# Causal attention with relative keys and a mixture of experts: skewed-key reads moved behind the next quad's write, keys 14 steps ahead, expert weights loaded one at a time

## The chip, the cores and the metric

The kernel runs on one core of one Trainium2 chip. The metric is device time in microseconds (us), lower is better. The core has a matrix engine (PE, its weight loads PEld), a vector engine (DVE), an activation engine (ACT), GpSimd (POOL) and a sync engine (SP), which here issues every DMA of the program, one after another, in the order of its program.

## What is computed

One pre-norm transformer block in fp32, over x of 8 x 512 x 128, with 16 heads of 8 elements:

```python
qkv = x @ w_attn                                   # x is the layer norm of the input
rel = jnp.tril(idx[:, None] - idx[None, :])        # distance t - s, 0 above the diagonal
att = einsum('bhtd,bhsd->bhts', q, k) * scale + einsum('bhtd,tsd->bhts', q, embk[rel])
att = softmax(where(causal, att, -inf))
y = einsum('bhts,bhsd->bhtd', att, v) + einsum('bhts,tsd->bhtd', att, embv[rel])
x = x + y @ w_proj
x = x + ffn(layernorm(x))   # softmax gate, 2 of 8 experts, and 2 shared experts
```

The tables embk and embv have 128 rows, so a distance over 127 takes row 127. The last row of each table is taken out of the tables and put into k and v beforehand, and only the near 128 distances are left to a special path.

## The kernel before

**The work.** A first part normalises x and makes q, k and v of all batches in four groups, and writes them to HBM as bf16 parts (`qk_rows`) and fp32 values (`v_dram`). Then comes attention, until about 610 us, then the expert layer (`expert_part`) to the end.

**Attention.** Four pairs of batches are worked through. Each has four rows of 128 queries, in the order ROWS = [2, 0, 1, 3]; row i sees (i+1) x 128 keys. A row of a pair has 32 heads, in 8 quads of 4 heads, so there are 128 quads, q = 0 to 127. A quad is cut into steps (UNITS): 1 head per step in rows 2 and 3, 2 in row 1, 4 in row 0, so a quad has 4, 1, 2 and 4 steps in rows 2, 0, 1 and 3, and there are 352 steps in all. `FIRST[q]` is the first step of quad q. I call the rows 2 and 3, with 4 steps a quad, the wide rows.

In a step m, PE transposes probabilities of step m-3 (L771), does whatever the table OPS holds for that step, and multiplies q by k for step m+1 (L759). DVE adds the near part to the scores of the step and takes their minimum in one instruction per head (L979, of the negated scores), ACT takes the exponential (L906). Copies of transposed probabilities go to ACT (L895) and DVE (L964) in turn. POOL, L720 and L724, folds the near probabilities, PE applies v (L788) and the relative values (L804).

**The near part, which the change is about.** For quad q:

1. PE multiplies q by the 128 relative keys (`rel`, L746) at step `REL_AT[q]`; ACT copies the product to SBUF (`rel_copy`, L884, 5 buffers).
2. SP writes it to HBM, `put_rel`, issued at L628: 256 KB into one of 8 slots with a pitch that is off by one element per partition. That skews it.
3. SP reads it back from the slot, `get_near`, issued at L636: 512 KB (256 KB in row 0) into one of NEAR = 5 buffers. Ahead of this DMA, SP waits for the write of the same quad to have landed (`w_out`), and for the buffer to be free (quad q-5 done on DVE).
4. The first L979 of quad q on DVE waits until the read has landed.

`rel_slots` sets how many steps the relative keys run ahead: 8 in rows 0 and 1, 10 in rows 2 and 3. `READ_AT` sets the step at which SP's program has the read. SP has no clock of its own: it goes through the steps m, and in each does first the reads of that step, then the writes, then other DMAs (rows of the first part, q, k and v of the next pair, residuals, stores). What paces it are its waits: a write waits until ACT has copied the product, a read until its own write has landed.

**Weights.** `load_weights` (L1127) issues the gate, its bias and w1, w3, w2 of the experts, 640 KB each, in one go, 8 steps after quad 32, the first of the second pair. They are first used in the expert layer.

Of the kernel before, what the change touches and what calls it, by code (L numbers as in the profile page):

```python
# [16 lines left out]
NI = T // P  # L17
# [9 lines left out]
QUADS = NH // 4  # L27
# [14 lines left out]
NQ = GI * QUADS  # L42
NEAR = 5
RSLOTS = 5
WSLOTS = 8
PROBS = 5
MINS = 32
MISC = 3
MISC_BANK = 5
# [7 lines left out]
FIRST = [UNITS.index((q, 0)) for q in range(NQ)] + [NU]  # L57


def row(q):  # L60

    return ROWS[q // QUADS % NI]
# [15 lines left out]
def rel_slots():  # L78

    at = []  # L80
    for q in range(NQ):
        ahead = 8 if row(q) <= 1 else 10
        reload = last(q - QUADS) + 4 if q // QUADS % NI == 0 and q >= QUADS else 0
        at.append(max(reload, FIRST[q] - ahead, *at[-1:]))
    return at
# [64 lines left out]
OPS, BANK, BEFORE, LAST = schedule()  # L150
SLOT_OF = {op: m for m in range(SLOTS) for op in OPS[m]}
REL_AT = [SLOT_OF["rel", q] for q in range(NQ)]
READ_AT = [max(REL_AT[q] + 3, FIRST[max(q - NEAR + 1, 0)]) if REL_AT[q] else 0 for q in range(NQ)]


def on_act(m):
# [333 lines left out]
def attention_part(nc, t, x, w_attn, w_proj, e_k, e_k127, e_k127h, e_v, e_v127, part_of_row, qk_rows, v_dram, w_slots,  # L490
                   x1_dram, experts_of):
    with ExitStack() as ctx:
# [31 lines left out]
        experts = experts_of(ctx, t, ps_all)  # L524
# [63 lines left out]
        with nc.Block() as block:  # L588

            @block.sync  # L590
            def _(sp):
# [23 lines left out]
                def load_v(g):  # L615
                    if g >= 2:
                        sp.wait_ge(av_done, NI * QUADS * (g - 1))
                    sp.dma_start(vb[:, g % 2, :, :], v_dram[:, g * GB * NI:(g + 1) * GB * NI, :]).then_inc(v_in[g % 2], 16)
# [53 lines left out]
                for m in range(SLOTS):  # L672
                    for q in range(NQ):
                        if READ_AT[q] == m > 0:
                            get_near(q)
                    for q in range(NQ):
                        if REL_AT[q] == m > 0:
                            put_rel(q)
                    for k in range((m - 2) * 3 // 2, (m - 1) * 3 // 2):
                        if 0 <= k < 2 * (2 * NPART + 1):  # L680
                            first["rows"](sp, 2 + k // (2 * NPART + 1), [k % (2 * NPART + 1)])
                    for q in range(NQ):
                        if m == last(q) + 1 and q // QUADS % NI == NI - 1 and q // QUADS // NI + 1 < G:
                            load_qk(q // QUADS // NI + 1, q % QUADS)
                        if m == last(q) + 8 and q % (NI * QUADS) == 0 and q // QUADS // NI + 1 < G:
                            if q == 0:
                                sp.wait_ge(*first["second_rows"])
                            elif q == NI * QUADS:
                                first["wait_rows"](sp)
                                experts["weights"](sp)  # L690
                            load_v(q // QUADS // NI + 1)
                    for e in range(GI - 1):
                        if m == SLOT_OF["yt", e, 0]:
                            load_residual(e)
                        if m == SLOT_OF["pj", e] + 3:
                            store(e)
                    if m == FIRST[NQ - QUADS]:
                        sp.wait_ge(av_done, NI * QUADS * (G - 1))
                        for j in range(3):
                            wait_stored(sp, j)  # L700
                            experts["load"](sp, j)
# [344 lines left out]
def expert_part(nc, ctx, t, ps, x1_dram, gate_w, gate_bias, w1, w3, w2, out):  # L1046
# [8 lines left out]
    w1_sb = w1_v.rearrange("p (m c) -> p m c", m=NM)  # L1055
# [24 lines left out]
    w_in = sem("w2_in")  # L1080
# [41 lines left out]

        return [j for j in range(1, CHUNKS) if prepared_at(j)[what] == step]

    def load_weights(sp):
        for dst, src in ((gw, gate_w), (gb, gate_bias), (w1_sb, w1), (w3_sb, w3), (w2_sb, w2)):
            sp.dma_start(dst, src).then_inc(w_in, 16)  # L1127

    def load_tokens(sp, j):
        sp.dma_start(x1c[j % 3], x1_tiles[:, CT * j:CT * (j + 1), :]).then_inc(x1c_in[j % 3], 16)  # L1130
# [312 lines left out]
```

## Time and profile before

| | before |
|---|---|
| time, median of 3 runs | 851.3 us (845.1 to 855.38) |
| the profiled execution | 854.7 us, of which the span is 853.0 us |
| PE busy | 717.1 us, 84% of the span |
| DVE / ACT / POOL busy | 70% / 60% / 30% |
| data moved | 140.32 MB, 164 GB/s over the span |
| attention steps | from about 60 to about 610 us |
| expert layer | from about 612 to 853 us |

The busy time of PE is that of pipelined matmuls and is not a measure of PE at its peak. An engine with idle time before an instruction has the name of what ended the wait beside it. SP's rows are issues of DMAs; a transfer itself goes on after its issue.

### The profile page before, as it was taken

The page shows a single profiled execution, that of the slowest core. Times are in us where ns is not written, and L with a number is a line of the kernel's source. Part 1 is how long each engine was busy: PE and PEld are TensorE (multiplying, and loading weights), DVE is VectorE, ACT ScalarE, POOL GpSimd, SP SyncE. Part 2 cuts the span into 40 slices and gives each one's busy share as a digit, 9 for nine tenths or more (in the row PEclk, how much of TensorE's full clock was granted, in tenths as well). Part 3 has the DMA queues.
Part 4 walks back from the last instruction along what each step waited for, and adds up shares of the span by engine and source line. Part 5 has one row for each costly group of instructions (what it writes and reads, how often), then busy time and mean ns, then how long its engine had stood idle before and what let it go on. Part 6 is the DMA issues. An engine that isn't in the chain of part 4 may idle for free. (4 is left out here: it accounts for less than half of the span.)

```text
span 853.0 us, 27128 instructions
## 1 busy us (share of the span) xinstructions
PE 717.1 (84%) x10368; PEld 522.4 (61%) x10368; DVE 594.8 (70%) x2036; ACT 512.4 (60%) x1031; POOL 255.2 (30%) x253
## 2 busy tenths in 40 slices
PE   3667569898597888877989777988799999999998
PEld 2345447676465766655768565767666666666665
DVE  6835458878477696767778657867746767766776
ACT  2565478687486685877768667758733434534331
POOL 8333236433235442435534333543300000000000
PEclk9877799999999898999999999989979999999999
DMA  9789989677788667569767658864200000000000
GB/s 312 235 277 286 351 259 273 183 211 207 233 244 241 188 181 215 169 202 290 220 170 217 180 159 250 259 190 128 74 2 20 25 26 25 13 13 13 13 13 13
DMA packets 116687, 140.32 MB, mean 164 GB/s; under 512 B 8848, under 2 KB 83088, under 8 KB 116368
## 3 DMA queue, kind: packets, MB, share of 16 engines
q1 hardware_dynamic: 116560, 138.59, 53.9%
q8 instruction: 84, 1.38, 0.7%
q14 instruction: 43, 0.35, 0.1%
HBM read 82.26 MB, written 56.30 MB: 162 GB/s over the span
## 5 line engine op out<-in xcount | busy, mean ns | idle before, releaser
L979 DVE CUSTOM_DVE_ANT_0 ps<-ps,near 128x128 f32<-128x128 f32 (+3 forms) x512 | 241.6, 510 | 146.3 <-PE ps L759 77.0
L906 ACT ACTIVATE work<-ps,nmin 128x128 f32<-128x128 f32 (+3 forms) x512 | 246.3, 539 | 112.7 <-DVE nmin L979 107.0
L771 PE MATMUL ps<-ident,work 128*128 128x128 f32 x1280 | 213.1, 288 | 20.8 <-issue 19.9
L771 PEld LDWEIGHTS ps<-ident,work 128*128 128x128 f32 x1280 | 158.7, 147 | 55.9 <-issue 34.7
L759 PE MATMUL ps<-kb,qb 128*128 128x128 bf16 (+3 forms) x512 | 134.2, 315 | 42.6 <-ACT work L906 36.3
L720 POOL TENSOR_SCALAR_AFFINE_SELECT work<-work 128x512 f32<-128x512 f32 x96 | 60.9, 635 | 299.9 <-ACT work L895 297.3
L1298 ACT ACTIVATE near<-ps 128x512 f32<-128x512 f32 x80 | 47.6, 595 | 137.1 <-PE ps L1263 137.0
L724 POOL TENSOR_TENSOR work<-work 128x512 f32<-128x512 f32 x96 | 124.0, 1292 | 8.0
L964 DVE COPY work<-ps 128x512 f32<-128x512 f32 (+1 forms) x192 | 122.8, 639 | 5.2 <-PE ps L771 4.2
L788 PE MATMUL ps<-work,vb 128*9 128x128 f32 x2560 | 101.4, 287 | 4.0 <-ACT relS L884 2.5
L1273 PEld LDWEIGHTS ps<-work,near 128*128 128x128 f32 x640 | 82.6, 192 | 34.3 <-issue 31.7
L884 ACT ACTIVATE relS<-ps 128x512 f32<-128x512 f32 x128 | 83.8, 656 | 23.3 <-PE ps L746 23.1
L895 ACT ACTIVATE work<-ps 128x512 f32<-128x512 f32 (+1 forms) x160 | 89.9, 562 | 12.8 <-PE ps L771 12.5
L1318 DVE TENSOR_TENSOR near<-near,ps 128x512 f32<-128x512 f32 x80 | 54.9, 686 | 54.0 <-ACT near L1298 34.4
L1263 PE MATMUL ps<-near,work 128*128 128x512 f32 x160 | 83.7, 605 | 0.0
L1273 PE MATMUL ps<-work,near 128*128 128x128 f32 x640 | 83.1, 275 | 0.0
L1264 PE MATMUL ps<-near,work 128*128 128x512 f32 x160 | 82.6, 598 | 0.0
L759 PEld LDWEIGHTS ps<-kb,qb 128*128 128x128 bf16 x512 | 43.7, 100 | 58.6 <-ACT work L906 44.7
L788 PEld LDWEIGHTS ps<-work,vb 128*9 128x9 f32 x2560 | 59.1, 93 | 31.0 <-issue 24.7
L1333 DVE SCALAR_TENSOR_TENSOR near<-ps,near 128x128 f32<-128x128 f32 x256 | 71.9, 343 | 5.5
L979 DVE DVE_READ_ACCUMULATOR2_ANT nmin<- 128x1 f32 x512 | 71.5, 140 | 0.0
L804 PE MATMUL ps<-tv,work 128*32 128x8 f32 x4096 | 52.2, 181 | 16.6 <-issue 16.6
(101 smaller groups left out, 653.3 us busy)
## 6 DMA issues: line engine op xcount, KB each, us to landing
near<-w_slots SPq DMA_DIRECT2D x96, 512.0 KB, 4.4
w_slots<-relS SPq DMA_DIRECT2D x128, 256.0 KB, 4.9
qk_rows<-work SPq DMA_DIRECT2D x48, 256.0 KB, 5.3
near<-w_slots SPq DMA_DIRECT2D x32, 256.0 KB, 5.0
w_slots<-near SPq DMA_DIRECT2D x8, 512.0 KB, 6.2
qb<-qk_rows SPq DMA_DIRECT2D x24, 96.0 KB
kb<-qk_rows SPq DMA_DIRECT2D x24, 96.0 KB
qb<-qk_rows SPq DMA_DIRECT2D x48, 48.0 KB
```

The source lines that it names most:

```text
L724: nc.gpsimd.tensor_tensor(dst, ptmp[:, :, :], pT[:, q % 2, :, i * P:(i + 1) * P], ALU.add).then_inc(pc_done, 1)
L759: ins = nc.tensor.matmul(qk_ps[:, m % 3, h * wide:(h + 1) * wide], qb[:, n, i * P:(i + 1) * P], kb[:, n // 4 * 2 + n % 2, 0:wide], start=T ...
L771: ins = nc.tensor.transpose(tp_ps[:, m % 2, n * P:(n + 1) * P], prob[:, m % PROBS, n * P:(n + 1) * P], ident[:, :])
L788: ins = nc.tensor.matmul(bank[32 * h:32 * h + VD, a * P:(a + 1) * P], vb[:, g % 2, b * NI + j, n * VD:(n + 1) * VD], pT[:, q % 2, h, j * P ...
L884: nc.scalar.activation(relS[:, q % RSLOTS, :, :, :].rearrange("p a j h -> p a h j"), misc("rel", q).rearrange("p (a h j) -> p a h j", a=2, ...
L895: nc.scalar.activation(pT[:, q % 2, n * w:n * (w + 1), 0:wide], tp_ps[:, m % 2, 0:n * wide].rearrange("p (h s) -> p h s", h=n), ACT.Copy). ...
L906: ins = nc.scalar.activation(prob[:, m % PROBS, h * wide:(h + 1) * wide], qk_ps[:, m % 3, h * wide:(h + 1) * wide], ACT.Exp, bias=nmin[:, ...
L964: nc.vector.tensor_copy(pT[:, q % 2, n * w:n * (w + 1), 0:wide], tp_ps[:, m % 2, 0:n * wide].rearrange("p (h s) -> p h s", h=n)).then_inc( ...
L979: nc.vector.tensor_tensor_reduce(out=scores, in0=scores, in1=near[:, q % NEAR, a, 4 * P - wide:4 * P, r], scale=1.0, scalar=3e38, op0=ALU. ...
L1263: nc.tensor.matmul(h1_ps[k % 2], w1_sb[:, m, :], rhs, start=True, stop=True).then_inc(h1_ready, 1)
L1264: nc.tensor.matmul(h3_ps[k % 2], w3_sb[:, m, :], rhs, start=True, stop=True).then_inc(h3_ready, 1)
L1273: ins = nc.tensor.matmul(y_ps[k % 2][:, n * P:(n + 1) * P], hT[:, (NM * c + m) % 4, n * P:(n + 1) * P], w2_sb[:, m, :], start=(m == ms[0]) ...
```

## The change

Three things are changed.

- Relative keys of rows 2 and 3 are made 14 steps ahead in place of 10, from quad 8 on (in the first 8 quads it stays 10).
- The read of a quad stands 5 steps after its write's in place of 3, in rows 2 and 3. A wide quad has 4 steps, so the read comes behind the next quad's write in SP's program instead of ahead of it.
- The five loads of expert weights are issued one by one at the first steps of quads 48 to 52, which are in row 1 of the second pair.

```diff
@@ rel_slots
-        ahead = 8 if row(q) <= 1 else 10
+        ahead = 8 if row(q) <= 1 else 10 if q < QUADS else 14
@@
-READ_AT = [max(REL_AT[q] + 3, FIRST[max(q - NEAR + 1, 0)]) if REL_AT[q] else 0 for q in range(NQ)]
+READ_AT = [max(REL_AT[q] + (3 if row(q) <= 1 else 5), FIRST[max(q - NEAR + 1, 0)]) if REL_AT[q] else 0
+           for q in range(NQ)]
@@ SP's program
                             elif q == NI * QUADS:
                                 first["wait_rows"](sp)
-                                experts["weights"](sp)
                             load_v(q // QUADS // NI + 1)
+                    for k in range(WEIGHTS):
+                        if m == FIRST[QUADS * (NI + 2) + k]:
+                            experts["weights"](sp, k)
@@ load_weights
-        for dst, src in ((gw, gate_w), (gb, gate_bias), (w1_sb, w1), (w3_sb, w3), (w2_sb, w2)):
-            sp.dma_start(dst, src).then_inc(w_in, 16)
+        dst, src = ((gw, gate_w), (gb, gate_bias), (w1_sb, w1), (w3_sb, w3), (w2_sb, w2))[k]
+        sp.dma_start(dst, src).then_inc(w_in, 16)
```

What this does to SP's program is seen in three places. The first is row 2 of the second pair, where the weights stood. `w_slots<-relS` is the write of a quad's skewed keys, `near<-w_slots` the read; each read there is of the quad whose write stands last above it. Before:

```order
155 L636 DMA near<-w_slots 128x2x512
156 L628 DMA w_slots<-relS 128x2x256
157 L636 DMA near<-w_slots 128x2x512
158 L628 DMA w_slots<-relS 128x2x256
159 L1127 DMA work<-in_gate_w 128x8
160 L1127 DMA work<-in_gate_bias 128x8
161 L1127 DMA work<-in_w 128x1280 x3
162 L618 DMA vb<-v_dram 128x1152
163 L636 DMA near<-w_slots 128x2x512
164 L628 DMA w_slots<-relS 128x2x256
```

The same place of the changed program (its lines stand 2 to 4 further down, so L638 is L636 and L630 is L628):

```order
153 L638 DMA near<-w_slots 128x2x512
154 L630 DMA w_slots<-relS 128x2x256
155 L638 DMA near<-w_slots 128x2x512
156 L630 DMA w_slots<-relS 128x2x256
157 L638 DMA near<-w_slots 128x2x512
158 L620 DMA vb<-v_dram 128x1152
159 L630 DMA w_slots<-relS 128x2x256
160 L638 DMA near<-w_slots 128x2x512 x2
```

Reads and writes alternate in both, but a read is now of the quad whose write stands one further up: row 155 reads what the write above row 154 wrote, not what row 154 writes. The weights are gone from here, the load of v has stayed.

The second place is SP's program in the first row of the first pair, where rows of q and k of the later batches (`qk_rows<-work`, 256 KB each) are written between the near transfers. The first row below is the write of quad 3. Before:

```order
28 L628 DMA w_slots<-relS 128x2x256
29 L279 DMA qk_rows<-work 128x2x512 x4
30 L636 DMA near<-w_slots 128x2x512
31 L279 DMA qk_rows<-work 128x2x512 x2
32 L628 DMA w_slots<-relS 128x2x256
33 L279 DMA qk_rows<-work 128x2x512 x4
34 L636 DMA near<-w_slots 128x2x512
```

And in the changed program:

```order
28 L630 DMA w_slots<-relS 128x2x256
29 L281 DMA qk_rows<-work 128x2x512 x6
30 L630 DMA w_slots<-relS 128x2x256
31 L281 DMA qk_rows<-work 128x2x512
32 L638 DMA near<-w_slots 128x2x512
33 L281 DMA qk_rows<-work 128x2x512 x5
34 L630 DMA w_slots<-relS 128x2x256
35 L276 DMA v_dram<-work 128x1152
36 L638 DMA near<-w_slots 128x2x512
```

The read of quad 3 (row 30, now row 32) has got three more rows of q and k and the write of quad 4 ahead of it.

The third place is where the weights now stand, in SP's program of the changed kernel in row 1 of the second pair, around quads 50 to 55 (the near reads here are still of the write last above them):

```order
186 L1131 DMA work<-in_gate_bias 128x8
187 L638 DMA near<-w_slots 128x2x512
188 L630 DMA w_slots<-relS 128x2x256
189 L1131 DMA work<-in_w 128x1280
190 L638 DMA near<-w_slots 128x2x512
191 L645 DMA xr<-in_x 128x2x128
192 L630 DMA w_slots<-relS 128x2x256
193 L1131 DMA work<-in_w 128x1280
194 L638 DMA near<-w_slots 128x2x512
195 L630 DMA w_slots<-relS 128x2x256 x2
196 L1131 DMA work<-in_w 128x1280
197 L638 DMA near<-w_slots 128x2x512
```

Each of the three large loads stands right ahead of one near read. On PE and ACT the relative keys of rows 2 and 3 come one wide quad earlier: they shift by 4 steps, so they keep their place beside the same kind of step, and only the first two quads of each row 3 crowd into the end of row 1 (steps 135 and 136 in the second pair, where they stood at 135 and 138).

## Rows read from the trace of the kernel before

**Rows 1.** Waits, whole span: engine line <- waited for: us in total, times, longest
```profile
ACT work L906 <- DVE nmin L979: 107.0, 79, 7.1
DVE ps L979 <- DMA near<-w_slots: 67.7, 37, 7.9
PE ps L759 <- ACT work L906: 36.3, 23, 7.0
```

**Rows 2.** By stretch: length; busy PE, PEld, DVE, ACT, POOL; clock, DMA share, GB/s
```profile
62.70:114.50 51.80, 36.13 (x341) 25.32 (x343) 24.45 (x80) 29.98 (x62) 15.49 (x16) 0.76 0.94 300
154.00:201.30 47.30, 42.03 (x812) 33.14 (x802) 39.21 (x110) 36.40 (x68) 18.22 (x20) 1.00 0.70 206
201.30:249.30 48.00, 35.72 (x664) 26.99 (x663) 28.08 (x94) 31.30 (x66) 16.33 (x17) 0.93 0.70 212
264.00:296.00 32.00, 25.71 (x738) 21.19 (x727) 21.40 (x82) 20.59 (x49) 14.31 (x15) 0.89 0.70 206
344.70:385.30 40.60, 33.94 (x663) 25.88 (x663) 27.86 (x93) 31.06 (x66) 16.32 (x17) 1.00 0.65 196
432.00:474.00 42.00, 39.73 (x745) 31.84 (x747) 36.63 (x100) 34.41 (x63) 16.91 (x18) 0.99 0.72 204
474.30:518.80 44.50, 33.06 (x638) 25.16 (x631) 28.11 (x93) 30.24 (x64) 15.41 (x17) 1.00 0.61 176
```

**Rows 3.** Waits of SP's own queue, whole span
```profile
SPq L636 <- DMA w_slots<-relS: 210.2, 93, 7.4
```

**Rows 4.** Timeline of ACT in row 2 of the fourth pair: start, us, line
```profile
483.09 0.72 ACT L884 ACTIVATE relS<-ps 128x512 f32<-128x512 f32 x1
```

**Rows 5.** Timeline of SP in the same row
```profile
488.59 0.55 SPq L628 DMA_DIRECT2D w_slots<-relS  x1
493.43 0.53 SPq L636 DMA_DIRECT2D near<-w_slots  x1
494.05 0.55 SPq L628 DMA_DIRECT2D w_slots<-relS  x1
498.70 0.53 SPq L636 DMA_DIRECT2D near<-w_slots  x1
```

**Rows 6.** Waits of DVE in the same row, 474.3 to 518.8 us
```profile
DVE ps L979 <- DMA near<-w_slots: 11.1, 6, 3.1
```

**Rows 7.** DMA issues: tiles, count, KB each, median us from issue to landing
```profile
near<-w_slots SPq DMA_DIRECT2D x96, 512.0 KB, 4.4
w_slots<-relS SPq DMA_DIRECT2D x128, 256.0 KB, 4.9
work<-in_w SPq DMA_DIRECT2D x3, 640.0 KB, 7.6
```

**Rows 8.** Timeline of SP where the weights are issued
```profile
219.80 1.46 SPq L1127 DMA_DIRECT2D work<-in_w  x3
...
224.34 0.53 SPq L636 DMA_DIRECT2D near<-w_slots  x1
```

**Rows 9.** Timeline of DVE, first instruction of quad 37
```profile
232.65 0.57 DVE L979 CUSTOM_DVE_ANT_0 ps<-ps,near 128x384 f32<-128x384 f32 x1 [7.87 <-DMA near<-w_slots]
```

**Rows 10.** Timeline of SP in the first row of the first pair
```profile
74.48 0.53 SPq L636 DMA_DIRECT2D near<-w_slots  x1
...
76.81 4.34 SPq L279 DMA_DIRECT2D qk_rows<-work  x4
82.20 0.53 SPq L636 DMA_DIRECT2D near<-w_slots  x1
```

**Rows 11.** The page's slices: GB/s moved in 40 equal parts of the span
```profile
GB/s 312 235 277 286 351 259 273 183 211 207 233 244 241 188 181 215 169 202 290 220 170 217 180 159 250 259 190 128 74 2 20 25 26 25 13 13 13 13 13 13
```

**Rows 12.** Waits of DVE in row 3 of the third pair, 432 to 474.3 us
```profile
DVE ps L979 <- DMA near<-w_slots: 1.3, 2, 1.1
```

**Rows 13.** Timeline of SP, read of quad 53 (row 1, second pair)
```profile
276.00 0.53 SPq L636 DMA_DIRECT2D near<-w_slots  x1
```

**Rows 14.** Timeline of DVE, first instruction of quad 53
```profile
282.77 0.42 DVE L979 CUSTOM_DVE_ANT_0 ps<-ps,near 128x256 f32<-128x256 f32 x1
```

More of the change, by code:

```diff
@@ L46 @@
 PROBS = 5
+WEIGHTS = 5
 MINS = 32
@@ L1123, in due, with load_weights @@
         return [j for j in range(1, CHUNKS) if prepared_at(j)[what] == step]
-    def load_weights(sp):
-        for dst, src in ((gw, gate_w), (gb, gate_bias), (w1_sb, w1), (w3_sb, w3), (w2_sb, w2)):
-            sp.dma_start(dst, src).then_inc(w_in, 16)
+    def load_weights(sp, k):
+        dst, src = ((gw, gate_w), (gb, gate_bias), (w1_sb, w1), (w3_sb, w3), (w2_sb, w2))[k]
+        sp.dma_start(dst, src).then_inc(w_in, 16)
     def load_tokens(sp, j):
```

## Prediction

> **What bounds the kernel now.** I read the waits of the whole span first. They form a chain: DVE's near addition waits 67.7 us for the read of skewed keys, ACT's exponentials wait 107.0 us for DVE, PE's products 36.3 us for ACT [rows 1]. So some DMA wait gets through to PE, the busiest engine. The 67.7 us are no gain to be had: part of them is made good before PE runs dry, and 36.3 us, which has waits of other origin in it too, is about what PE loses.
>
> The stretches by row come next. In row 3 PE is busy 42.03 of 47.3 us and 39.73 of 42.0 us, 89% and 95%, at a clock of 1.00 and 0.99; nothing is to be had there. In row 2 it is busy 33.94 of 40.6 us, 84%, and 33.06 of 44.5 us, 74%, at a clock of 1.00, and 35.72 of 48.0 us at 0.93 [rows 2]. In the last 44.5 us DVE waited 11.1 us for near reads [rows 6].
>
> SP's queue says why a read is late. SP stands 210.2 us in front of near reads, waiting for the quad's own write to land [rows 3]. Row 2 of the fourth pair shows one round. ACT finished the copy of a quad's keys at 483.8, and its write was issued only at 488.59: for 4.8 us the data was ready and SP was standing in front of the read before it. The write took until 493.43, when the read went out, and the next write followed at 494.05 [rows 4, 5]. A round is thus issue of the write, its landing, issue of the read: 494.05 − 488.59 = 5.5 us, the next 498.70 − 493.43 = 5.3 us. A write's landing, 4.9 us at the median, fills it [rows 7]. This round, one quad long, is slower than the engines: PE's 33.94 us for 8 quads are 4.2 us a quad [rows 2]. In row 3 the engines need 42.03 / 8 = 5.3 us of PE and more with DVE, so the same round hides there. In row 2 SP's round sets the pace.
>
> **The change part by part.**
>
> *Read behind the next write.* SP now issues write q+1 and then waits for write q, issued a quad earlier. If writes land 4.9 us after issue and a quad takes 4.5 us, nearly all of the landing is over when SP comes to the read. Two quads now share one landing: write q+2 goes out right behind read q, and so one landing and one issue, 4.9 + 0.6 us, after write q. That is 2.7 us a quad, below every engine. The order excludes a loss of free buffers: reads wait for quad q−5, and in wide rows that one is through 16 steps before quad q starts, the read stands 9 before.
>
> *14 steps in place of 10.* The read of q has the copy of q+1 as its condition, which lies 10 steps ahead of use, as the copy of q did before. Ten steps are two and a half wide quads, 10.5 us at 4.2 us each; a read lands in 4.4 us [rows 7], so about 6 us of slack remain, where before it was 10.5 − 4.9 − 4.4 = 1.2 us, gone after one round of 5.3 us. That slack also covers the load of v in row 2. The added work is nothing: as many products, copies and transfers as before. ACT and PE take two copies and products earlier at the end of row 1; at 0.72 us a copy [rows 4], on engines busy 20.59 and 25.71 of 32 us there [rows 2], I cost it at 0; without that cover it would be 0.7 us in each of four pairs.
>
> *Row 2 of pairs 2 to 4.* They take 48.0 + 40.6 + 44.5 = 133.1 us. With PE busy 33.94 us at clock 1.00, at row 3's shares of 95% and 89% a row comes to 35.7 and 38.2 us. I take 38.0, near the upper end, because its last 8 steps carry the relative keys of row 0, one per step, with 0.72 us of ACT each. 133.1 − 3 × 38.0 = 19.1 us. Bounds: 133.1 − 3 × 35.7 = 26; with 1.5 us more a row, if row 0's first read, still 8 steps ahead, comes late, 133.1 − 3 × 39.7 = 14. The weights' share is in this: issued at 219.80, they held up a read issued at 224.34 until DVE had waited 7.87 us for it [rows 8, 9].
>
> *The first row.* It takes 51.8 us, with DMA engines 94% busy at 300 GB/s and a clock of 0.76 [rows 2]: half of its trouble is bandwidth. For quad 3 the change is a loss: its read went out at 74.48 [rows 10], and now has three rows of q and k and one write, 4 × 256 KB, in front: 1.05 MB at 300 GB/s, 3.5 us. After that the gain outweighs it, since writes go out when their copies are made and not a landing later. SP's rounds there, 74.48 to the next read at 82, are 7 to 8 us of which 4.3 us is a stalled issue of four rows [rows 10]; that stall stays. It gives between 0 and what the best slice's 351 GB/s would [rows 11], 51.8 × (1 − 300/351) = 7.5 us. I take 4.
>
> *Row 3.* The third pair's waits 1.3 us for reads [rows 12]; over the pairs I take 2 us.
>
> *Weights in row 1.* Three loads of 640 KB, each right in front of a near read, the first of them of quad 53. That read went out at 276.00, lands in 4.4 us and was used at 282.77 [rows 7, 13, 14]: slack 2.4 us. One load is 0.66 MB, at the 300 GB/s of a full stretch 2.2 us, so its read is late by a fraction: −1 us for all three. Upper bound: a full landing of 7.6 us [rows 7] each, less that slack, 3 × 5.2 = 16 us. The DMA engines have room there, with 206 GB/s and a share of 0.70 [rows 2].
>
> **A rule weighed.** A write takes 4.9 us to land by the row. The Trainium skill, DMA: Bandwidth & Descriptors, section on the anatomy of one DMA, gives for DMAs issued by GpSimd about 2.0 us and bytes over 436 GB/s, which for 256 KB would be an estimate of 2.6 us. With the issues' 0.6 us a round of SP would be 3.2 us, under the 4.2 us of PE, and the reordering would be worth nothing. The traced rounds of 5.3 to 5.5 us contradict it here, where SP issues.
>
> **Sum.** 19.1 + 4 + 2 − 1 = 24.1 us. The profiled execution, 854.7 us, becomes 830.6. It lies 3.4 us over the median of 851.3; the same step from there gives 827.2. I predict 827. The expert layer is untouched.
>
> **The rivals.**
>
> *The engines take over early.* DVE, ACT and PE hand work to each other, and PE may not get past 89% in row 2; row 0, whose keys stay 8 steps ahead, starts late; the first row gives 0. Then 133.1 − 3 × 39.7 = 14, less a larger price of 4 for the weights: 10 us, 841. For it: the 3.5 us at quad 3 and row 0's bandwidth. Against it: row 2 idles in front of reads, not of engines.
>
> *The wait moves from SP into the DMA engines.* With a write and a read in flight at once, each may take longer, as in the first row, where the DMA share was 0.94. If the read needed 10.5 us instead of 4.4, DVE would wait as before: 851. For it: SP waited up to 7.4 us for one write [rows 3]. Against it: row 2 has a share of 0.61 to 0.70 and 176 to 212 GB/s [rows 2], against 300 in the first row. The Trainium skill's formula gives this same result, no change, by the other route, that the landing was never the pace.
>
> *Slower: weights in row 1.* A near key passes the queue twice, as a write and as a read. If each load of 640 KB holds up both by its 7.6 us [rows 7], each costs 15.2 less 2.4 us of slack, 12.8 us, three cost 38, and 25 − 38 leaves the kernel 13 us slower, 864. It eats the whole gain from 10.7 us a load on. Against it: the loads' 7.6 us is for three in flight together, and 2 MB more over 32 us is 61 GB/s more than 206. The Trainium skill's same page, DMA: Bandwidth & Descriptors, section on queues, rings and completion order, has descriptors of one ring consumed in order, so that a read behind a load starts after it; that gives the order of this rival, not its price.
>
> *More than forecast.* In the first row the clock was 0.76 [rows 2], so half of that time PE ran at 1.2 GHz, with 30% of it idle. If PE is fed more evenly and stays at 2.4 GHz, the first row could come to 43 us, 5 more than taken, and row 2 to 36.5: 34 us, 817.
>
> **How the numbers follow.** Forecast (gain 15 to 32 us) 0.66; more 0.07; engines early 0.16; wait moved, or never the pace, 0.07; weights 0.04. The range reaches from 817, the larger gain, less 2 for the scatter of the runs, to 842, the small one: 815 to 842. About 1%, 8.5 us, is what a measurement of this kernel can tell. Faster by more than that is the forecast, the larger gain and two thirds of the small one: 0.83. Within 1%: the rest of the small one and the moved wait: 0.13. Slower: 0.04.
>
> **What would show it.** In the changed profile SP's wait in front of near reads for their writes falls from 210 us to under 100; DVE's wait for near reads falls from 67.7 to under 30 us, what is left lying in the first row and in rows 0; each later row 2 takes 36 to 39.5 us with PE over 85% busy; the write goes out within 1 us of ACT's copy. Quad 3 starts about 3 us later and quad 8 about 4 us earlier. At the new place of the weights a DVE wait of about 1 us appears. The prediction is wrong if row 2 keeps its 40 to 48 us with DVE waiting for reads (the DMA engines), or with PE waiting for ACT or DVE without reads behind it (the engines), or if row 1 of the second pair grows by over 5 us.

## The result and the profile after

The changed kernel takes 823.25 us at the median of 4 runs (822.32 to 827.82), the kernel before, on the same chip, 852.41 us (4 runs, 845.1 to 855.38). The ratio is 0.968, with a 95% interval of 0.961 to 0.975, so the change gains 29 us. The forecast was 827 us with a range of 815 to 842. The profiled execution took 822.64 us, its span is 820.8 us. The experiments below were timed in three groups, each beside the kernel before, whose medians were 847.4, 858.4 and 853.6 us; each experiment is compared by its ratio to the kernel before of its own group. Medians are of all runs, while a ratio and its interval use only the fast runs, those within 1.5% of a kernel's fastest, so the two can differ a little. In two of the groups the changed kernel was timed again, with ratios of 0.958 and 0.969; that is how far one and the same kernel moves.

The waits of the whole span after the change, in the form of [rows 1] (L983 is the near addition L979, L910 the exponential L906, L763 the product L759, all moved down by 4 lines):

```profile
ACT work L910 <- DVE nmin L983: 79.2, 73, 5.1
DVE ps L983 <- DMA near<-w_slots: 26.2, 15, 5.4
PE ps L763 <- ACT work L910: 14.5, 10, 4.9
```

The chain of waits has shrunk at each link: DVE's from 67.7 to 26.2 us, ACT's from 107.0 to 79.2, PE's from 36.3 to 14.5. Of DVE's 26.2 us, 17.1 lie in the first row, 5.5 in the rows 0 and 3.6 in row 1 of the first pair. SP's queue has turned over. Where it stood 210.2 us in front of reads, waiting for a landing [rows 3], it now mostly waits for ACT to have a product ready:

```profile
SPq L630 <- ACT relS L888: 155.7, 79, 8.5
SPq L638 <- DMA w_slots<-relS: 70.7, 46, 5.5
```

The same place as [rows 4] and [rows 5], row 2 of the fourth pair, first ACT, then SP:

```profile
459.14 0.72 ACT L888 ACTIVATE relS<-ps 128x512 f32<-128x512 f32 x1
```

```profile
459.89 0.36 SPq L630 DMA_DIRECT2D w_slots<-relS  x1
460.56 0.53 SPq L638 DMA_DIRECT2D near<-w_slots  x1
463.25 0.36 SPq L630 DMA_DIRECT2D w_slots<-relS  x1
464.01 0.53 SPq L638 DMA_DIRECT2D near<-w_slots  x1
467.17 0.36 SPq L630 DMA_DIRECT2D w_slots<-relS  x1
```

ACT is done at 459.86 and the write goes out at 459.89, where it had been 4.8 us late. Writes follow each other after 3.4 and 3.9 us instead of 5.3 to 5.5, at the pace of the engines.

The stretches by row, columns as in [rows 2]. They are the first row, row 2 of the second pair, rows 0 and 1 there, row 2 of the third pair, row 3 of the third, row 2 of the fourth:

```profile
63.60:111.40 47.80, 32.90 (x320) 23.04 (x318) 24.73 (x80) 28.01 (x58) 13.92 (x15) 0.81 0.98 325
199.00:238.50 39.50, 34.53 (x659) 26.91 (x659) 28.22 (x94) 30.65 (x65) 16.31 (x17) 0.96 0.65 201
238.50:252.50 14.00, 12.20 (x229) 8.30 (x227) 12.40 (x76) 11.64 (x38) 6.41 (x7) 1.00 0.91 268
252.50:289.40 36.90, 30.06 (x715) 23.82 (x715) 23.00 (x89) 22.51 (x54) 15.87 (x16) 0.81 0.78 249
333.80:368.70 34.90, 33.16 (x659) 25.51 (x659) 27.99 (x94) 30.61 (x65) 16.34 (x17) 1.00 0.73 226
412.00:452.40 40.40, 37.98 (x704) 30.40 (x704) 36.40 (x100) 33.18 (x60) 16.33 (x18) 1.00 0.76 224
452.40:489.40 37.00, 33.29 (x659) 25.68 (x659) 28.05 (x94) 30.58 (x65) 16.31 (x17) 1.00 0.65 201
```

I measured every row like this, from the first near addition of the row to that of the next, and summed the four pairs of each kind:

| | before | after | difference |
|---|---|---|---|
| row 2, first pair | 51.8 | 47.7 | −4.1 |
| row 2, pairs 2 to 4 | 48.0 + 40.6 + 44.5 = 133.1 | 39.5 + 34.9 + 37.0 = 111.4 | −21.7 |
| row 0, all pairs | 63.6 | 57.7 | −5.9 |
| row 1, all pairs | 126.4 | 131.4 | +5.0 |
| row 3, all pairs | 173.9 | 169.8 | −4.1 |
| all after the last near addition | 241.7 | 239.1 | −2.6 |
| all before the first near addition | 62.7 | 63.6 | +0.9 |

Row 2 of the third pair is 95% PE now: 33.16 of 34.90 us. Each profile is of one execution. The stretch after the last near addition, nearly all of it the expert layer, is the same code in both kernels, and took 238.8 to 243.3 us in the other profiles, so its −2.6 us is scatter.

One remark of the description of the change has to be set right: in row 1 a near read is not of the write last above it, in either kernel. A quad has 2 steps there and the read stands 3 steps behind its write, so the next quad's write already goes out first. In the kernel before the read of quad 53 was issued at 276.00 [rows 13], and the write of quad 54 at 275.55 (SP of the kernel before). So row 1 already had the order that the change gives to rows 2 and 3, and in rows 1 of the kernel before DVE waited for no read.

### The profile page after: what moved, and what is told of

The parts are those of the page before. It is cut to its first block and busy times, and to the rows that moved or that the text cites. A ratio compares the mean times of both kernels' runs of the same rounds, so it can differ in the third digit from the quotient of the medians.

```text
span 820.8 us, 27128 instructions
## 1 busy us (share of the span) xinstructions
PE 705.1 (86%) x10368; PEld 514.0 (63%) x10368; DVE 594.8 (72%) x2036; ACT 512.0 (62%) x1031; POOL 255.2 (31%) x253
## 5 line engine op out<-in xcount | busy, mean ns | idle before, releaser
L983 DVE CUSTOM_DVE_ANT_0 ps<-ps,near 128x128 f32<-128x128 f32 (+3 forms) x512 | 242.7, 510 | 120.5 <-PE ps L763 93.2
L910 ACT ACTIVATE work<-ps,nmin 128x128 f32<-128x128 f32 (+3 forms) x512 | 249.3, 550 | 83.3 <-DVE nmin L983 79.2
L775 PE MATMUL ps<-ident,work 128*128 128x128 f32 x1280 | 209.4, 283 | 12.5 <-issue 11.1
L775 PEld LDWEIGHTS ps<-ident,work 128*128 128x128 f32 x1280 | 155.2, 145 | 49.1 <-issue 27.4
L763 PE MATMUL ps<-kb,qb 128*128 128x128 bf16 (+3 forms) x512 | 132.3, 311 | 22.8 <-ACT work L910 14.5
L1277 PEld LDWEIGHTS ps<-work,near 128*128 128x128 f32 x640 | 82.5, 192 | 34.3 <-issue 31.7
L792 PE MATMUL ps<-work,vb 128*9 128x128 f32 x2560 | 98.7, 283 | 3.8 <-ACT relS L888 3.7
L1322 DVE TENSOR_TENSOR near<-near,ps 128x512 f32<-128x512 f32 x80 | 54.9, 687 | 51.8 <-ACT near L1302 36.5
L1267 PE MATMUL ps<-near,work 128*128 128x512 f32 x160 | 82.8, 599 | 0.0
L1268 PE MATMUL ps<-near,work 128*128 128x512 f32 x160 | 81.7, 592 | 0.0
L808 PE MATMUL ps<-tv,work 128*32 128x8 f32 x4096 | 51.8, 180 | 26.1 <-issue 25.7
L983 DVE DVE_READ_ACCUMULATOR2_ANT nmin<- 128x1 f32 x512 | 72.8, 142 | 0.0
L808 PEld LDWEIGHTS ps<-tv,work 128*32 128x32 f32 x4096 | 48.9, 112 | 32.3 <-issue 30.2
```

Of the source, the lines that this page charges most:

```text
L763: ins = nc.tensor.matmul(qk_ps[:, m % 3, h * wide:(h + 1) * wide], qb[:, n, i * P:(i + 1) * P], kb[:, n // 4 * 2 + n % 2, 0:wide], start=T ...
L775: ins = nc.tensor.transpose(tp_ps[:, m % 2, n * P:(n + 1) * P], prob[:, m % PROBS, n * P:(n + 1) * P], ident[:, :])
L792: ins = nc.tensor.matmul(bank[32 * h:32 * h + VD, a * P:(a + 1) * P], vb[:, g % 2, b * NI + j, n * VD:(n + 1) * VD], pT[:, q % 2, h, j * P ...
L808: ins = nc.tensor.matmul(bank[32 * tq:32 * tq + NH, a * D:(a + 1) * D], pcT[:, e % 2, tau, :], tv[:, tau, :], start=True, stop=True)
L910: ins = nc.scalar.activation(prob[:, m % PROBS, h * wide:(h + 1) * wide], qk_ps[:, m % 3, h * wide:(h + 1) * wide], ACT.Exp, bias=nmin[:, ...
L983: nc.vector.tensor_tensor_reduce(out=scores, in0=scores, in1=near[:, q % NEAR, a, 4 * P - wide:4 * P, r], scale=1.0, scalar=3e38, op0=ALU. ...
```

## Experiments

**Each part alone.** The first three runs put one part of the change each into the kernel before, a fourth takes one out of the changed kernel.

*Weights alone.* The kernel before with this part only (moved to quads 48 to 52, as in the changed kernel):

```diff
-                                experts["weights"](sp)
+                    for k in range(WEIGHTS):
+                        if m == FIRST[QUADS * (NI + 2) + k]:
+                            experts["weights"](sp, k)
```

> The kernel before with the five weight loads moved alone to row 1 of the second pair. Theory (reads are late because SP alternates a write, its landing and a read, and the weights lay in front of one read): row 2 of the second pair loses the waits of 7.9 and 1.9 us and goes from 48.0 us to about 41 us, the other two later rows 2 keep their 40.6 and 44.5 us, row 1 of the second pair grows by 0 to 3 us; the time falls by 5 to 8 us, to about 845. Rival (a load in row 1 holds up the write and the read of near keys by its full 7.6 us): row 1 of the second pair grows by over 15 us and the kernel gets slower, to about 860.

Measured: 845.7 us at the median against 847.4 of the kernel before, ratio 1.004 with an interval of 0.997 to 1.012. No gain can be seen, against the 5 to 8 us that I had expected. In the profile the long wait was gone from row 2 of the second pair, which took 42.7 us in place of 48.0 (about 41 expected), but the profiled execution, 837.9 us, was the second fastest of the kernel's ten, and other rows, which the weights do not touch, differ by up to 4.3 us. What the profile does show is the pace. The three later rows 2:

```profile
202.70:245.40 42.70, 33.31 (x642) 25.22 (x634) 28.27 (x92) 30.55 (x64) 15.56 (x17) 1.00 0.67 198
335.50:377.90 42.40, 34.22 (x664) 25.90 (x663) 27.88 (x93) 31.25 (x66) 16.33 (x17) 1.00 0.65 196
461.90:504.10 42.20, 34.41 (x634) 26.30 (x631) 28.10 (x92) 30.21 (x64) 15.32 (x17) 0.96 0.64 183
```

42.7, 42.4 and 42.2 us: 8 quads of 5.3 us, although PE works 33 to 34 us in each. SP's timeline in the first of them has the same figure, 5.3, 5.3 and 5.0 us from write to write:

```profile
210.26 0.55 SPq L629 DMA_DIRECT2D w_slots<-relS  x1
...
215.56 0.56 SPq L629 DMA_DIRECT2D w_slots<-relS  x1
220.25 0.53 SPq L637 DMA_DIRECT2D near<-w_slots  x1
220.88 0.55 SPq L629 DMA_DIRECT2D w_slots<-relS  x1
...
225.88 0.55 SPq L629 DMA_DIRECT2D w_slots<-relS  x1
```

So the wait of 7.87 us at the weights [rows 9] was worth 5.3 us in the row itself, and there SP's pace stops the gain: 8 rounds of 5.3 us are 42.4 us. Part of the 5.3 us is the clock, 0.93 in that row before and 1.00 here. Why nothing of it shows in the medians is not known; the interval leaves room for 0.3%, under 3 us.

*Lead alone.* Keys 14 steps ahead, reads still ahead of the next write:

```diff
-        ahead = 8 if row(q) <= 1 else 10
+        ahead = 8 if row(q) <= 1 else 10 if q < QUADS else 14
```

> The kernel before with relative keys 14 steps ahead, reads still ahead of the next quad's write, weights in one go as before. Theory (SP's round of 5.3 us a quad is the pace, against 4.3 us of the engines): 4 more steps give about 4.3 us of slack once, which a row of 8 quads eats at 1 us a quad, so SP's writes still go out up to 4 us after ACT's copy, DVE's waits for reads in the later rows 2 fall from 33 to about 10 us, and the gain is 12 to 18 us, about 836. Rival (only the lead matters, the order nothing): DVE's waits in rows 2 are 0 as in the changed kernel, and it takes about 825. Second rival (only the order matters): under 4 us of gain.

Measured: 836.8 us, ratio 0.987 (0.983 to 0.991), a gain of 10.6 us, a little under the 12 to 18 us expected. The rows 2 took 45.9, 37.8 and 40.4 us. SP's rounds are unchanged, 5.2 us, and its lateness grows along a row. In row 2 of the fourth pair it goes from 2.8 to 6.3 us: at the end the copy is done at 478.77 and its write goes out at 485.02, 6.3 us late (ACT, then SP):

```profile
478.10 0.67 ACT L884 ACTIVATE relS<-ps 128x512 f32<-128x512 f32 x1
```

```profile
479.16 0.52 SPq L636 DMA_DIRECT2D near<-w_slots  x1
479.77 0.56 SPq L628 DMA_DIRECT2D w_slots<-relS  x1
484.40 0.52 SPq L636 DMA_DIRECT2D near<-w_slots  x1
485.02 0.93 SPq L628 DMA_DIRECT2D w_slots<-relS  x1
```

Yet DVE's waits for reads were 5.6 us in the second pair's row 2 and none in the other two, fewer than I had expected: four more steps of slack last just about as long as a row.

*Order alone.* Reads behind the next write, keys still 10 steps ahead:

```diff
-READ_AT = [max(REL_AT[q] + 3, FIRST[max(q - NEAR + 1, 0)]) if REL_AT[q] else 0 for q in range(NQ)]
+READ_AT = [max(REL_AT[q] + (3 if row(q) <= 1 else 5), FIRST[max(q - NEAR + 1, 0)]) if REL_AT[q] else 0
+           for q in range(NQ)]
```

> The kernel before with reads of wide rows behind the next quad's write alone, relative keys still 10 steps ahead, weights in one go as before. Theory (the round is the pace): SP waits no more for a full landing, writes go out within 1 us of the copy, but a read goes out only at the next quad's copy, 6 steps or 6.4 us ahead of use, and lands in 5.5 us: slack of 1 us. DVE's waits for reads in the later rows 2 fall from 33 to 5 to 12 us, most of them beside the weights and the load of v; the first row is as in the changed kernel, 48 us. Gain 14 to 20 us, about 834. Rival (only the lead matters): reads go out no earlier than before, DVE waits as before or more, and the time is 850 or more.

Measured: 829.2 us, ratio 0.978 (0.971 to 0.986), a gain of 18 us. SP's waits for landings fall to a third, from 210.2 to 62.3 us:

```profile
SPq L629 <- ACT relS L885: 175.6, 92, 8.5
SPq L637 <- DMA w_slots<-relS: 62.3, 41, 5.7
```

DVE's waits in the later rows 2 were 11.0, 6.2 and 4.8 us, 22 in all and more than I had expected. One of them, beside the weights in the second pair, is 6.6 us long and that row took 45.5 us; the others are 2.3 us or less, since a read that goes out 6 steps ahead just fails to be there. Row 2 of the fourth pair took 38.5 us with this in it:

```profile
460.10:498.60 38.50, 33.66 (x662) 25.90 (x662) 28.20 (x92) 31.22 (x65) 16.24 (x17) 1.00 0.70 212
```

So both parts work and neither is all of it. Order takes away the pace of 5.3 us; lead then gives each read time. Their gains, 2.2% and 1.3%, add up to about that of the whole. About 3 us of the order's gain lie in the first row, 48.6 us against 51.8, where the lead is the same.

*Weights put back.* The changed kernel with the five loads in one go at their old place:

```diff
                                 first["wait_rows"](sp)
+                                for k in range(WEIGHTS):
+                                    experts["weights"](sp, k)
                             load_v(q // QUADS // NI + 1)
-                    for k in range(WEIGHTS):
-                        if m == FIRST[QUADS * (NI + 2) + k]:
-                            experts["weights"](sp, k)
```

> The changed kernel with the five weight loads in one go at their old place, ahead of the load of v. Theory (lead and order give 4 to 6 us of slack there): the 2 MB hold up one read by about 7 us, of which DVE sees 0 to 3 us; row 2 of the second pair takes 39.5 to 42 us in place of 39.5, row 1 there loses 0 to 3 us; the time is that of the changed kernel within 2 us, 823. Rival (moving the weights carries a part of the gain of its own): the wait of 7.9 us is back, row 2 takes 47 us, and the time is about 831.

Measured: 818.6 us, ratio 0.963 (0.953 to 0.973), no loss. Since this group has no changed kernel of its own, the kernel was timed a second time, beside the changed kernel.

> The changed kernel as base of this call: 0.958 to 0.968 of the kernel before.

Measured for the base: 822.6 us, ratio 0.969 (0.961 to 0.977).

> The changed kernel with the weights in one go at their old place, once more, against the base of the same call. Theory (with 4 to 6 us of slack the place of the weights no longer matters): within 0.7% of the base, row 2 of the second pair 35 to 41 us with under 1 us of waits for reads, row 1 there 1 us shorter. Rival (moving them carries part of the gain): 1% slower than the base.

Measured: 822.9 us, ratio 0.970 (0.963 to 0.977), the same as the base. The profile shows both sides. At the old place one read is late:

```profile
232.24 0.57 DVE L982 CUSTOM_DVE_ANT_0 ps<-ps,near 128x384 f32<-128x384 f32 x1 [4.63 <-DMA near<-w_slots]
```

I had expected under 1 us here. That row 2 nonetheless took 39.3 us, against 39.5 in the first profile of the changed kernel, and row 1 of the pair took 31.7 us, against 36.9. How much of the latter is the weights' is taken up further down.

*Most of the weights left out.* The changed kernel, with a slice of w1, w3 and w2 in place of all:

```diff
-        dst, src = ((gw, gate_w), (gb, gate_bias), (w1_sb, w1), (w3_sb, w3), (w2_sb, w2))[k]
+        dst, src = ((gw, gate_w), (gb, gate_bias), (w1_sb[:, 0:1], w1[:, 0:1]), ...)[k]
```

> The changed kernel with only one column of w1, w3 and w2 of each expert... that is, the first column of 1280 loaded; the loads stay at their new places with all their issues and waits, but 2 MB are left out, so the expert layer computes with other numbers at the same cost. Theory (2 MB in row 1 cost about 1 us, hidden for the rest by slack): 0 to 2 us faster than the base, row 1 of the second pair 33 to 36 us. Rival (each load holds up near keys by its landing): row 1 there falls by over 5 us and the time by as much.

The slice is one of the 10 matrices of each, not one column as the expectation has it, so a tenth is loaded and 1.8 MB are left out. Measured: 820.0 us, ratio 0.967 (0.959 to 0.974), 2.7 us below the base and inside the scatter. Row 1 of the second pair took 33.9 us. A cost of the 2 MB at their new place can't be told from the scatter, and the row did not fall by the rival's 5 us.

**The first row.** The changed kernel, with the old order of reads in the first 8 quads:

```diff
-READ_AT = [max(REL_AT[q] + (3 if row(q) <= 1 else 5), ...
+READ_AT = [max(REL_AT[q] + (3 if row(q) <= 1 or q < QUADS else 5), ...
```

> The changed kernel with the old order of reads in the first 8 quads alone (read ahead of the next quad's write there). Theory (the first row is half bound by bandwidth, and the new order gains 4 us over its 8 quads after losing 3.5 us at quad 3): quad 3 starts at 79 us in place of 83, the first row takes 51 to 52 us in place of 47.7, all else stays; 4 us slower than the changed kernel of the same call. Rival (bandwidth alone sets the first row): it takes the same 48 us within 1 us with either order, and the total does not move.

Its base is the changed kernel of the same group:

> The changed kernel once more, on the same chip as the three others of this call, as their base: 0.968 of the kernel before, row 2 of the three later pairs 35 to 40 us each without waits for reads, first row 48 us.

Measured: 831.5 us, ratio 0.971 (0.964 to 0.978), against 819.4 us and 0.958 (0.951 to 0.965) for the base. The first rows, old order first:

```profile
62.70:115.80 53.10, 36.85 (x356) 26.32 (x355) 24.68 (x80) 30.55 (x62) 15.66 (x16) 0.77 0.93 295
```

```profile
62.60:111.30 48.70, 33.23 (x320) 23.37 (x319) 24.66 (x79) 28.27 (x59) 14.07 (x15) 0.81 0.98 322
```

The row is 4.4 us longer with the old order, and the DMA engines are less busy, 0.93 against 0.98. The clock differs as well, 0.77 against 0.81, and PE's idle time hardly does (16.3 and 15.5 us), so the clock could be the cause. Two other profiles speak against that. The first profile with the weights put back has the new order at a clock of 0.76, the one with the weights alone the old order at 0.80:

```profile
64.30:113.80 49.50, 34.65 (x329) 24.57 (x330) 24.77 (x79) 28.68 (x59) 14.40 (x15) 0.76 0.94 314
```

```profile
62.80:115.00 52.20, 35.68 (x357) 25.53 (x356) 24.67 (x79) 30.39 (x62) 15.71 (x16) 0.80 0.94 299
```

With 10 steps of lead the row takes 51.7 to 53.1 us in all four profiles with the old order and 47.7 to 49.5 us in all nine with the new. The order makes it shorter; whether through fuller DMA engines or a higher clock is not separated. Quad 3 is earlier with the old order and later with the new, as forecast (first old, then new):

```profile
79.89 0.57 DVE L983 CUSTOM_DVE_ANT_0 ps<-ps,near 128x384 f32<-128x384 f32 x1 [1.58 <-DMA near<-w_slots]
```

```profile
82.69 0.57 DVE L983 CUSTOM_DVE_ANT_0 ps<-ps,near 128x384 f32<-128x384 f32 x1 [5.77 <-DMA near<-w_slots]
```

The medians are 12 us apart. 4.4 of that is explained; the rest is no more than the two intervals allow.

*Lead of 14 in the first row too:*

```diff
-        ahead = 8 if row(q) <= 1 else 10 if q < QUADS else 14
+        ahead = 8 if row(q) <= 1 else 14
```

> The changed kernel with relative keys 14 steps ahead in the first 8 quads too. Theory (the first row waits 17 us for reads because 10 steps do not cover a write of 7.5 us, a read of 6 to 7.5 us and the rows of q and k between them): quad 3, whose write moves ahead of the loop, no longer waits, the waits fall to 8 to 12 us and the first row by 2 to 5 us. Rival (the DMA engines are full there, share 0.94): transfers only move, the first row stays at 47 to 50 us, no gain.

Measured: 825.0 us, ratio 0.965 (0.957 to 0.974), no gain over the base. DVE's waits for reads in the first row fell from 17.4 to 11.7 us, but its waits for PE grew from 7.0 to 14.4, and the row took 52.6 us, even longer than the rival had it. What made it longer is neither of the two. Quads 4 to 7 of the first row are of the second batch, and SP's program has the load of that batch's q (`qb<-qk_rows`) behind all writes and reads that stand ahead of the steps. With 14 steps those of quad 3 joined them, so the load went out at 66.39 us in place of 63.05, while the product of quad 4 stood at step 2 in place of 6. PE then stood still for the load, first in this kernel, then in the base:

```profile
75.71 0.61 PE L750 MATMUL ps<-te,qb 128*128 128x128 bf16 x4 [11.68 <-DMA qb<-qk_rows]
```

```profile
70.56 0.40 PE L750 MATMUL ps<-te,qb 128*128 128x128 bf16 x4 [2.61 <-DMA qb<-qk_rows]
```

These 9.1 us more of standing still, at a clock of 0.73 for the row, are more than the 3.9 us that the row is longer. So this run doesn't tell whether the lead or the DMA engines bound the first row.

**More of the same.** Keys 18 steps ahead and the read behind the write after the next one, each read still 9 steps ahead of use:

```diff
-        ahead = 8 if row(q) <= 1 else 10 if q < QUADS else 14
+        ahead = 8 if row(q) <= 1 else 10 if q < QUADS else 18
-READ_AT = [max(REL_AT[q] + (3 if row(q) <= 1 else 5), ...
+READ_AT = [max(REL_AT[q] + (3 if row(q) <= 1 else 5 if q < QUADS else max(5, min(9, FIRST[q] - 9 - REL_AT[q]))), ...
```

> The changed kernel with keys 18 steps ahead and reads behind the write after the next one, from quad 8 on in wide rows (each read still 9 steps ahead of use). Theory (the write's landing was the pace, and one quad of distance hides it): SP's waits for landings, 70.7 us, fall to under 45 us, DVE's waits for reads in later rows 2 stay 0, and the time is that of the changed kernel within 3 us. Rival (landings still cost something): 4 us or more faster.

Measured: 831.4 us, ratio 0.969 (0.962 to 0.976) against 0.958 of the base. SP's waits for landings fell only to 60.1 us, not under 45 (L638 of the base: 64.8). DVE waited for no read in the later rows 2 with either. Nothing is left there for a longer distance to hide; that it is 1% slower is at the edge of the intervals, and I have no cause for it.

*Keys of rows 0 and 1 at 10 steps:*

```diff
-        ahead = 8 if row(q) <= 1 else 10 if q < QUADS else 14
+        ahead = 10 if row(q) <= 1 or q < QUADS else 14
```

> The changed kernel with keys of rows 0 and 1 made 10 steps ahead in place of 8. Theory (row 0 waits 0.6 to 3 us a pair because a read there is held to 4 steps ahead of use by the 5 buffers, not by its keys): the waits of quads 4 to 7 of row 0 stay, only those of the first four go, row 0 changes by less than 1 us a pair, the time by under 3 us. Rival (the keys' lead bounds row 0 as it bound row 2): the waits in row 0 fall to 0 and the time by 4 us or more.

Measured: 815.2 us, ratio 0.961 (0.955 to 0.968), against 0.969 (0.961 to 0.977) of its base. This is the fastest median of its group, by 7.5 us, more than the 3 us that I had allowed; the intervals overlap and I don't count it as faster, but the rival's 4 us or more is not excluded either. In the profile the four rows 0 took 55.7 us, against 56.7 to 60.3 in the three profiles of the changed kernel, with waits for reads of 3.0, 1.3, 0.8 and 0.0 us. All that is left stands at quads 4 and 7 of a row 0, as it would if the 5 buffers held those reads; in the three profiles of the changed kernel the row 0 of the first pair has a wait at quad 3 too, of 1.2 to 2.2 us. A version that surely beats the changed kernel was not found.

## Why the prediction was right

**What bounds the kernel.** SP's round of write, landing and read set the pace of row 2. This is shown three times: by the rows 2 of 42.2 to 42.7 us in the weights-alone kernel, by the order alone, which gains 18 us with all else in place, and by the lead alone, in which SP goes on falling behind and the gain is 10.6 us. With the formula that the Trainium skill, DMA: Bandwidth & Descriptors, section on the anatomy of one DMA, gives for DMAs issued by GpSimd, a landing would have been hidden in a round of 3.2 us. It does not carry over to SP's writes here, which took 4.9 us at the median before and 4.3 after: had it held, the order alone would have been worth nothing.

**Row 2 of pairs 2 to 4.** 19.1 us forecast, 21.7 found. 38.0 us a row was too careful; PE came to 95% in one of them, not 89%, and to 87% and 90% in the others. The upper bound of 26 us stood, though one row, of 34.9 us, came out below the 36 to 39.5 us named as the sign. What makes a row longer is not what the prediction feared, the relative keys of row 0 in its last steps, which are in all of them. The row of 34.9 us has no stop of PE of the kind shown in the last section and a clock of 1.00; the row of 39.5 us has a stop of 3.3 us and a clock of 0.96, the row of 37.0 us a stop of 1.9 us. Later rows 2 without a stop at clock 1.00 take 34.6 to 35.9 us in every profile of the changed kernel and of its variants.

**The first row.** 4 us forecast, 4.1 found, and 4.4 between the two orders in the experiment. The 4 us had been picked between bounds of 0 and 7.5, so part of this is luck. The loss at quad 3 was put at 3.5 us; it was 3.6 (79.33 to 82.97 us), 1.0 of which the whole row started later, and 2.8 in the experiment, whose rows start together. The read itself went out only 0.8 us later (75.29 against 74.48): the bytes ahead of it made it land later, as forecast. That half of the row's trouble is bandwidth is not shown, since in the lead-14 run another wait came in between.

**Row 3.** 2 us forecast, 4.1 found in the profile. Only 2.4 us of that were waits for reads. The prediction had less room here than it took. Its stretch of 47.3 us [rows 2] begins 5 us ahead of row 3 of the first pair; the row itself is this one of the kernel before:

```profile
159.00:201.30 42.30, 38.26 (x701) 30.28 (x699) 36.38 (x100) 33.22 (x60) 16.30 (x18) 1.00 0.72 212
```

That is 4.8 us of PE a quad, not 5.3, and so less than a round of SP. That the round hid in row 3 is borne out by the short waits there, not by this sum.

**Weights in row 1.** −1 us forecast. DVE waited for no read there, where a wait of about 1 us was expected, but the row grew from 33.7 to 36.9 us, and was 36.3 us in the second profile of the changed kernel, against 31.7 us with the weights back at their old place. In the seven profiles with 14 or 18 steps and the weights at the new place the row took 34.0 to 37.0 us, in the three with the weights put back or mostly left out 31.7, 33.9 and 35.1 us, so up to 2 or 3 us may be theirs. Two other things differ by as much. The row in the kernel before, in the changed kernel's second profile and with the weights back:

```profile
264.40:298.10 33.70, 27.41 (x717) 22.44 (x712) 22.81 (x88) 21.94 (x54) 15.95 (x16) 0.90 0.68 201
```

```profile
247.00:283.30 36.30, 27.01 (x726) 21.68 (x717) 22.71 (x87) 22.14 (x53) 15.61 (x16) 0.95 0.78 250
```

```profile
257.80:289.50 31.70, 26.76 (x714) 21.25 (x715) 22.68 (x88) 22.15 (x54) 15.92 (x16) 0.95 0.71 221
```

In the changed kernel's first profile the clock was 0.81 in this row. The clock time not granted, by an estimate (1 − 0.81) × 36.9 = 7.0 us, is 3.6 us more than before and 5.4 us more than with the weights back, about as much as the rows differ. The second profile had the clock of 0.95 and took long all the same, with 8.2 us of stops of PE against 2.4 us with the weights back. Whether the weights have to do with either is not shown.

In the time it can't be told: 822.6 against 822.9 us. What was wrong in this step is the room in the DMA engines, which I read from the mean of the row. The three loads went out at 266.0, 269.0 and 272.0 us, and the read behind the first landed just before DVE used it. From 270 to 280 us the DMA engines were full, and a write took 8.0 us to land. The DMA view of that stretch:

```profile
q1 hardware_dynamic: 2096, 3.68, 102.0%
near<-w_slots SPq DMA_DIRECT2D x4, 512.0 KB, 6.3
w_slots<-relS SPq DMA_DIRECT2D x3, 256.0 KB, 8.0
work<-in_w SPq DMA_DIRECT2D x1, 640.0 KB, 8.9
```

That is the landing time that the slower rival had assumed, 7.6 us for the load and as much for the keys. I put it down to two things, without a run that shows it, that this didn't cost 38 us: the three loads lay in one congestion, not three, and its writes were those of row 3's first quads, which had 9 steps and more until their use.

**The weights' old place.** The prediction booked the wait of 7.87 us [rows 8, 9] to the gain of row 2. That part of the sum was right for a wrong share: alone, the move shortens that row in the profile but gains nothing that can be measured in the time, and undone it costs nothing. It was the 4 to 6 us of slack and the new pace that made row 2 faster.

**What the sum left out.** Row 0 gained 5.9 us, which stood nowhere in it; DVE's waits for reads in rows 0 fell from 14.5 to 5.5 us. SP came out of row 2 behind time before; at the first quad of row 0 in the third pair the copy was done at 374.16 and the write went out at 376.01 (ACT and SP of the kernel before). After the change it is 358.31 and 358.33 (ACT and SP of the changed kernel):

```profile
373.50 0.66 ACT L884 ACTIVATE relS<-ps 128x512 f32<-128x512 f32 x1 [0.28 <-PE ps L746]
```

```profile
376.01 2.15 SPq L628 DMA_DIRECT2D w_slots<-relS  x3
```

```profile
357.66 0.65 ACT L888 ACTIVATE relS<-ps 128x512 f32<-128x512 f32 x1 [0.28 <-PE ps L750]
358.33 1.83 SPq L630 DMA_DIRECT2D w_slots<-relS  x2
```

Row 1 gave 5.0 us back. I had costed the two quads of keys that come early there at 0, or 0.7 us a pair. The three profiles with keys 10 steps ahead have 126.4, 125.0 and 126.9 us in rows 1, and the nine of the changed kernel and the experiments with 14 or 18 that can be compared 129.9 to 137.2. So this step was mis-sized, by 3 us at least. It goes with the longer lead, and the weights are not all of it, since lead alone has 129.9. By what it comes is not shown: part of it is PE standing still in front of L808, L804 before, for nothing that the profile shows (16.6 us before, 25.7 after), but with lead alone that is 17.7 us, so it doesn't come from the lead by itself.

These two errors cancelled, and that is luck. The sum of the parts came to 24.1 us, the measured gain was 29, and of the profiled executions 32, of which 2.6 us are the scatter of the expert layer. The mechanism was right and carries about 22 us of the gain in the profile; that the forecast came within 4 us of the time is in part chance.

## What to carry over

A queue that issues a transfer, waits for it and then issues the next one has a pace of its own, a landing plus its issues (5.3 us here, with the DMA engines only 0.64 to 0.67 busy); put the next write between a write and the read that waits for it, and compare the round with the engines' time for the same unit of work. Lead and order do different things: order changes the pace, lead pays once for lateness that a slow pace brings back, so a longer lead alone hid the slow queue here for about a row. A single long wait in a trace can be worth less than its length: the pace around it and other waits take their share, so ask what the row would have taken without it before booking it. And before a row's growth is laid to a change, look at the clock and at the stops of PE in it; here they were as large as what was to be explained.

## What the runs showed of the hardware

A write of 256 KB that took 4.9 us from issue to landing at the median [rows 7] took 4.3 us in the changed kernel, and a read of 512 KB 5.5 in place of 4.4 us, with the same bytes over a shorter time. The sum of both hardly moved. The order-alone kernel has 4.0 and 5.0 us, lead alone 4.7 and 4.5 us. The shift comes with the order: where a read is issued behind the next write, writes land sooner and reads later.

PE stood still in the middle of a run of small matmuls, with nothing in the profile to wait for, for up to 3.3 us. One of them (PE of the changed kernel):

```profile
274.23 0.35 PE L808 MATMUL ps<-tv,work 128*32 128x8 f32 x18
277.81 0.82 PE L808 MATMUL ps<-tv,work 128*32 128x8 f32 x46 [3.23 <-issue]
```

Between the first near addition and 620 us there are 19 such stops of 0.8 us or more before, 31 us in all, and 20 after, 35 us. Most end 1.9 to 3.3 us after the start of a packet of 16 KB on the instruction queue (q8), 14 of the 19 and 18 of the 20; but there are over 70 such packets in that time, so most go by without such a stop. What triggers the stops was not tried; no change of SP's order removed them, and they are as large as all that was gained here.

Stretches at half the clock, 1.2 GHz in place of 2.4, follow some of these stops. In the changed kernel PE stood still until 277.81, and the granted clock was 0.50 from 276.3 us on, the figure behind POOL's:

```profile
276.30:283.10 6.80, 5.29 (x93) 4.57 (x96) 3.27 (x14) 1.44 (x3) 0.39 (x2) 0.50 1.05 353
```

In the kernel before it was 0.50 from 231.6 to 238.3 us, where the wait of 7.87 us [rows 9] ended at 232.65.
